# Storing eleven small moment rows to DRAM as BF16 from GpSimd instead of as F32 from SyncE, in a layer norm, state-space and ternary FFN kernel

## What is computed

```python
xn = layernorm(x)
# attention part, on xn
mu, var = mean(xn), mean((xn - mu)**2)
u  = (xn - mu) / sqrt(var + 1e-5) * ln_gamma + ln_beta
dt = exp(log_dt)
dA = exp(-exp(log_A) * dt[:, None]);  dB = B_param * dt[:, None]
h  = dA * h + dB * u_t[..., None]                  # scan over t
y_t = einsum('dn,bdn->bd', C_param, h) + D_param * u_t
attn = xn + y @ W_out.T + b_out
# ffn part, on xn: ternary(w) = clip(round(w / mean|w|), -1, 1)
ffn = gelu(xn @ ternary(W1).T + b1) @ ternary(W2).T + b2
out = x + attn + ffn
```

## Time and profile before

| | us |
|---|---|
| median of 2 runs | 1133.51 (1132.79 and 1134.22) |
| the profiled execution, own time | 1132.87 |
| its span on the slowest core (core 2) | 1131.3 |
| spans of the 8 cores | 1123.1 to 1131.3 |

### The profile page before, as it was taken

The page is one execution under the profiler, slowest core; times in us unless marked ns, Lnnn a source line. Parts: engine busy times, 40 slices in busy tenths (PEclk is TensorE's granted clock), DMA queues, the critical chain, the costliest instruction groups (busy, mean ns, idle before and its releaser), DMA issues. The chain is left out here.

```text
span 1131.3 us, 11756 instructions; the slowest of 8 cores (1123.1 to 1131.3 us)
## 1 busy us (share of the span) xinstructions
PE 747.6 (66%) x3553; PEld 321.4 (28%) x3622; DVE 430.2 (38%) x825; ACT 390.4 (35%) x481; POOL 99.4 (9%) x193
## 2 busy tenths in 40 slices
PE   0012222100999899709888888889329999999996
PEld 0000000000222222104444444444214444444442
DVE  3578888692444434512223232322101211212212
ACT  0033333201344344227888888887310000000000
POOL 1000000231111111110111111110000000000000
PEclk9999999999999999958999999999659999999999
DMA  4111111125655566434555555553563544245420
GB/s 72 39 37 56 56 56 56 14 24 107 186 167 168 157 186 168 123 82 142 177 177 169 176 186 177 168 185 132 148 174 87 149 112 133 75 128 149 117 70 38
DMA packets 78637, 136.43 MB, mean 121 GB/s; under 512 B 11448, under 2 KB 44656, under 8 KB 78576
## 3 DMA queue, kind: packets, MB, share of 16 engines
q0 software_dynamic: 19536, 63.42, 20.0%
q1 hardware_dynamic: 38304, 55.47, 16.0%
q10 hardware_dynamic: 20736, 16.79, 5.5%
HBM read 114.59 MB, written 25.21 MB: 124 GB/s over the span
## 5 line engine op out<-in xcount | busy, mean ns | idle before, releaser
L1182 PE MATMUL ps_c<-W2T,hgrp 128*128 128x512 bf16 x500 | 113.1, 382 | 15.3 <-DMA hgrp<-scr_h 14.7
L691 ACT ACTIVATE wabs<-wch 128x512 f32<-128x512 f32 x128 | 79.4, 628 | 125.9 <-DMA wch<-L_ffn_W 73.8
L1182 PE MATMUL ps_e<-W2T,hgrp 128*128 128x512 bf16 x498 | 111.9, 379 | 0.7
L541 PE MATMUL ps_d<-sb_cID,xnb 128*128 128x128 bf16 x128 | 16.2, 306 | 140.6 <-ACT xnT L454 86.1
L788 PE MATMUL ps_c<-ub,sb_cP 128*128 128x512 bf16 x60 | 19.8, 460 | 86.4 <-DVE ub L714 83.5
L1182 PEld LDWEIGHTS ps_c<-W2T,hgrp 128*128 128x128 bf16 x512 | 50.4, 99 | 75.9 <-issue 16.5
L226 POOL DMA_DIRECT2D wch<-L_ffn_W x96 | 51.5, 537 | 206.8 <-ACT wabs L691 169.0
L1182 PEld LDWEIGHTS ps_e<-W2T,hgrp 128*128 128x128 bf16 x512 | 50.1, 98 | 60.4
L709 DVE TENSOR_TENSOR ub<-xn2sb,mtb 128x512 bf16<-128x512 bf16 x128 | 45.7, 419 | 43.6 <-DMA mtb<-scr_mrow 20.4
L1028 PE MATMUL ps_a<-xnT,w1st 128*128 128x512 bf16 x250 | 61.2, 386 | 0.5 <-issue 0.2
L1028 PE MATMUL ps_b<-xnT,w1st 128*128 128x512 bf16 x248 | 60.8, 383 | 0.4
(11 more groups left out here) (147 smaller groups left out, 1054.3 us busy)
## 6 DMA issues: line engine op xcount, KB each, us to landing
wch<-L_ffn_W SPq DMA_DIRECT2D x64, 256.0 KB, 3.6
wch<-L_ffn_W POOLq DMA_DIRECT2D x64, 256.0 KB, 4.2
wch<-L_ffn_W POOLq DMA_DIRECT2D x32, 512.0 KB, 5.6
wchC<-L_ffn_W POOLq DMA_DIRECT2D x32, 512.0 KB, 4.9
scr_h<-hst SPq DMA_DIRECT2D x32, 512.0 KB, 2.9
xt<-x SPq DMA_DIRECT2D x16, 512.0 KB, 3.4
hgrp<-scr_h SPq DMA_DIRECT2D x128, 64.0 KB, 4.6
hgrp<-scr_h ACTq DMA_DIRECT2D x128, 64.0 KB, 4.8
```

The lines of the kernel that those rows point to most:

```text
L541: inst = te.transpose(ps_d[:, dblk * 128:(dblk + 1) * 128], xn_b[p][:, dblk * 128:(dblk + 1) * 128], cID[:, :])
L691: ac.activation(wabs[j % 4][:, :], wchunk[wk % 2][:, h * 512:(h + 1) * 512], AF.Abs).then_inc(s_wa, 1)
L1182: te.matmul(pso[:, sl], hgrp[tg % 2][:, fc * 256 + tk * 128: fc * 256 + (tk + 1) * 128], W2T[:, fc * 1024 + dh * 512: fc * 1024 + (dh + 1) ...
```

## The change

`scr_mrow` becomes a BF16 tensor. The eleven stores of `mom` move from SyncE to GpSimd and become casts, and their stream is `cst` instead of `ld`. The two waits of GpSimd for the moment stores (in B2 and B3) wait for `cst` accordingly. The variable `b0b_cst`, for which VectorE and TensorE wait at the start of B1, is taken behind the stores, so that its value now takes them in (5 DMAs before, 16 now). The loads of the moment rows in B2 and B3 are the same lines, but source and destination are now both BF16: 2 KB are read for each 2 KB written, where it was 4 KB.

```diff
-    scr_mrow = nc.dram_tensor("scr_mrow", [NMOM, D], F32)
+    scr_mrow = nc.dram_tensor("scr_mrow", [NMOM, D], BF16)
...
-            @blk.sync
-            def _(sy):
-                sy.wait_ge(s_dv, b0b_dv)
+            @blk.gpsimd
+            def _(gp):
+                gp.wait_ge(s_dv, b0b_dv)
                 for k in range(NMOM):
-                    sdma(sy, "ld", bass.AP(scr_mrow, k * D, [[8, 128], [1, 8]]),
+                    sdma(gp, "cst", bass.AP(scr_mrow, k * D, [[8, 128], [1, 8]]),
                          mom[:, k * 8:(k + 1) * 8])
-            b0b_ld = streams["ld"]["n"]
 
             b0b_cst = streams["cst"]["n"]
...
             @blk.gpsimd
             def _(gp):
-                swt(gp, "ld", b0b_ld)
+                swt(gp, "cst", b0b_cst)
                 gp.wait_ge(s_dv, b2_dv1)
...
             @blk.gpsimd
             def _(gp):
-                swt(gp, "ld", b0b_ld)
+                swt(gp, "cst", b0b_cst)
                 if debug_taps:
```

## The result

The kernel after takes 1140.8 us (median of 33 runs) beside 1132.9 us of the kernel before (31 runs): the ratio is 1.0065, with a 95% interval from 1.005 to 1.0081, so the change costs 7.4 us (5.7 to 9.2). The ratio leaves out a few executions in a slower state of the chip, which the medians take in, so it gives 7.4 us and not the 7.9 between the medians. The forecast was 1131.3 us in a range up to 1135.2. The profiled execution after took 1143.2 us.

The account below looks back on a forecast made before the run. VectorE was taken as the busy engine early, TensorE later, with three VectorE waits as the change's field. Stores +1.3, B2 loads -0.1 and B3 loads -3.4 gave -2.2 us: 1133.5 to 1131.3 us, range 1129.0 to 1135.2.

Parts of the forecast that it names:

- The term of the stores: End of B0b: moving the eleven stores to GpSimd costs +1.3 us, with bounds +0.7 to +2.
- Start and issuing of the stores: B0b: GpSimd starts 0.56 us after release (+0.47) and issues eleven stores in 5.89 us (+0.80).
- The barrier's 0.40 us (49.54 to 49.94) stays: End of B0b: the barrier between last store and x's issue keeps taking 0.40 us.
- I put the added wait at 0: Start of B1: VectorE and TensorE waiting for the stores' landing adds 0, as x's load covers it.
- The loads: B2 and B3: reading BF16 rows saves 0.1 us in B2 and 3.4 us of the wait for mtb.
- No gain in the loads: Rival, B3: broadcast rows cost the same whatever their length, the wait stays 20.4 us; 1134.7 us, chance 0.13.
- The stores land late: Rival, B1: each casting store packet costs 0.216 us, VectorE waits 9.2 us more; 1140.5 us, chance 0.06.
- the sign I gave for it: Start of B1: VectorE's first operation released by scr_mrow would show the late-stores rival, chance 0.06.
- the other: B3: a wait for mtb staying above 19 us would show the rival without gain in the loads, chance 0.13.
- x issued near 51.2 us: End of B0b: sign of the forecast, x issued near 51.2 us and VectorE going on near 56.4.

Follow-up runs that it names:

- e7: Kernel before plus six large casting loads of W1 rows by GpSimd in B0b, data unused: 1138.2 us in one run.
- e2: Kernel after with block B0b ending without GpSimd's drain, the barrier by semaphores alone: 1137.14 us, ratio 1.0051 to the kernel before.
- e5: Kernel after with scr_mrow left F32, so GpSimd stores 32-byte pieces without a cast: 1133.95 us, ratio 1.0036 to the kernel before.
- e11: Kernel after with each partition writing 16 elements (32 bytes) per casting store, values loaded not the moments in order: 1133.36 us, ratio 0.9996.
- e1: Kernel after with GpSimd's stores at the start of B1, VectorE and TensorE there waiting for constants only: 1123.71 us, ratio 0.9941.
- e10: Kernel before plus a BF16 copy of the scratch by one casting GpSimd DMA in B1, which the loads read: 1129.87 us, ratio 0.9978.
- e4: Kernel before with SyncE waiting in B0b until its own eleven F32 stores have landed: 1131.98 us, ratio 1.0016.
- e12: Kernel before plus GpSimd casting stores of 16-byte pieces 32 bytes apart into a scratch nobody reads: 1137.9 us (3 runs), ratio 1.0067.
- e9: Kernel before with F32 stores moved to GpSimd in B1, then one casting DRAM copy to BF16 for the loads: 1123.08 us, ratio 0.9919.
- e6: Kernel before with BF16 scratch: VectorE makes a BF16 copy of the moments, SyncE stores 16-byte pieces without a cast: 1138.8 us, ratio 1.0071.
- e3: Kernel after with VectorE and TensorE waiting at B1's start for the constants only, not the stores: 1136.45 us, ratio 1.0061 to the kernel before.
- e8: e1 with GpSimd issuing the stores only after VectorE has normalized the first tile: 1126.75 us, ratio 0.9962 to the kernel before.

## Why the prediction was wrong

The sum was +1.3 - 0.1 - 3.4 = -2.2 us. Measured, by VectorE's waits, it was +9.2 - 0.2 - 2.8 = +6.2. The term of the stores is the one that failed, in two steps.

**Start and issuing of the stores: right.** 0.56 us from release to first issue and 5.77 us for eleven were forecast at 0.56 and 5.89.

**"The barrier's 0.40 us (49.54 to 49.94) stays": this step failed first.** Those 0.40 us were measured with SyncE's DMAs in flight and none of GpSimd's. With GpSimd's, the block's end waits for their landing (after, e7; gone in e2), 6.65 us on core 2. The description of the kernel before says that a DMA which was only issued need not have landed at a barrier; for GpSimd's DMAs that is not so. Where I looked, the trace of before did not show it. In B0 too GpSimd's DMAs are in flight, but its last one, `sb_cID`, is issued at 3.8 us and lands 13.3 us later, at 17.1, ahead of TensorE's first operation at 17.95, so a wait for it has nothing to hold. I took "no row" for "no price". Even with quick landing this costs: e5's idle is +2.0 us where +1.3 was forecast.

**"I put the added wait at 0": the step that failed by the larger amount.** Its argument was the packets' time, 9 and 36 ns. That was right (21 ns), and it was the wrong quantity: the landing came 4.5 us or more after the last packet. The 1.7 us that it allowed for the landing were those of a load; stores of 32 bytes keep them (e5, e11), stores of 16 bytes do not. It was also applied to the wrong waiter. I allowed the stores until 56.4 - 1.7 = 54.7 us because x's load covered them; but the drain stands ahead of x's load, so nothing covers them. The price split, by VectorE's idle: 12.1 - 10.3 = 1.8 us for 32-byte pieces through GpSimd (e11), 19.56 - 12.14 = 7.4 more for pieces of 16 bytes. In time, after stands 1.0065 to e11's 0.9996, which agrees: 7.8 us.

The Trainium skill (DMA: Bandwidth & Descriptors, "Specifications") has it that a transfer below 512 bytes becomes a read-modify-write. I set the rule aside because F32 stores, below 512 bytes too, cost 9 ns. The runs agree with it only in part: 32-byte pieces land flat in 1.7 us, whether cast (e11) or not (e5), and those of 16 bytes pile up at 8 to 9 ns each in after, though not in e1. What in the writing makes that difference the runs do not show.

**The loads: right.** B2 gave -0.2 for -0.1. The wait for `mtb` gave -2.8 us on the mean (2.9 on core 2) for -3.4, with two rows in a packet as forecast; in e10, without the stores' trouble, the end came 2.5 us earlier. Between runs this wait differs by more than the difference to 3.4: with BF16 rows it is 14.4 us (e1) to 18.4 (e11) as a mean over the cores, with F32 rows 19.2 (e4) to 21.4 (e12). The mean of the nine profiles with BF16 rows is 16.3, of the five with F32 rows 20.0, which makes -3.7. The Trainium skill (DMA: Bandwidth & Descriptors, "Anatomy of one DMA") gave an estimate of 2.4 us for it, nearer to the 2.8 of the one pair and farther from the 3.7 of all profiles than the rows' 3.4.

**The rivals.** "No gain in the loads" falls with e10. "The stores land late" named 1140.5 us at a chance of 0.06, and 1140.8 came. That is luck, for its mechanism was another: it had each packet hold an engine for 0.216 us until 65.6 us, and VectorE wait for the stores. Measured are 21 ns a packet, a last landing at 55.5 us on core 2, and the drain as the waiter. So the sign I gave for it (VectorE's first operation released by `scr_mrow`) did not show, and neither did the other on core 2 or on the mean (a wait for `mtb` above 19 us; cores 0 and 1 had 19.1 and 19.8), and the forecast was wrong all the same: both signs hung on my mechanisms. The one that would have served was also in the text, x issued near 51.2 us. It was issued at 56.15.

## What to carry to other kernels

In these programs a DMA that GpSimd has issued is part of the block in which it is issued: unless its drain is left out (e2), the block's end waits for the landing, so issue it at the start of a block that computes, not at the end of one that does not. Judge a store by its landing, not by its packets, and before narrowing what is stored look at the length of a contiguous piece in DRAM: F32 to BF16 made 16 bytes of 32 here, and that cost 7.4 us where the narrower loads gave 2.8 (3.7 over all profiles). If the narrow form is wanted for the readers, store wide pieces and let one copy cast them off the path (e9).

## What the runs showed of the hardware

- GpSimd's drain at a block's end waits for the landing of its own DMAs, stores and loads: x is issued 0.5 to 0.8 us after the last landing in after and e7, and 4.3 us after the first store when the drain is left out (e2). SyncE's DMAs do not hold the block: x is issued 0.40 us after its last store in before, and in e6 too, where the packets of x then start only 5.5 us later.
- Eleven DMAs of 128 packed pieces of 16 bytes into DRAM, with nothing beside them, land late and later from one to the next: the last one 6.5 to 9.7 us after its issue in after (1.0 to 1.2 us per 128 pieces), 4.6 to 8.4 in e3. With 32 bytes every one takes 1.7 us (e5, e11). With 16 bytes at a distance of 32 bytes, and SyncE's stores beside them, the last one takes 3.4 to 4.1 us.
- Such pieces hold up loads that are issued behind or beside them: in e6 two tiles of x moved no packet for 5.2 us, while the DMA engines showed no work at all.
- Beside loads of x the 16-byte stores land after some 3 to 4 us on some cores and 7 to 9 on others, in e1 the odd ones, in e8 the cores 0, 3, 5 and 6. Why is open, and it was not tried.
